# A kernel of two phases: centring products moved between the halves of a convolution, and a pair's ranks, numbers and weights moved ahead of the second normalisation of the step

## The chip, the cores and the metric

The kernel runs on one core of a Trainium2 chip. The metric is the device time of one execution in microseconds (us). Before the change it is 1603.58 us, the median of 3 runs (1603.55 to 1603.79).

## What is computed

The input is 32 images of 128 channels and 32x32 pixels. In the order of the reference:

```python
x = x + conv(ln_c(x))        # ln_c: normalise over the 128 channels of each pixel
# conv: 3x3 depthwise, its nine weights for each image and channel are a softmax of
#   (max(x) @ w2.T + b2) - (mean(x) @ w1.T + b1); plus bias, plus its own input
t = tokens(x)                # 32 * 1024 tokens of 128 numbers
t = t + experts(ln_t(t))     # top 2 of 8 experts, 128 -> 512 -> gelu -> 128, weighted by a softmax of the two gate logits
x = images(t)
```

The softmax of the nine weights runs over an axis of length 1, and the kernel carries it out like that. The convolution and the routing fill the first third of the time and the experts nearly all of the rest.

## The kernel before, in words

**First phase: 19 steps over 16 pairs of images.** A pair goes through four stages, one step apart, so that a step works on up to four pairs: stage n of step s handles pair s - n + 1. Steps 3 to 15 have all four stages. Every engine has its own `step` function, and the order of the calls in it is the order of its work; nothing else schedules it. Engines meet through semaphores only. In what follows image 0 and image 1 are the two of a pair, and an image's 1024 pixels are treated as two halves of 512.

- Stage 1, normalisation. (The **mark** of a step, below, is the variance product of the second half of its image 1: once per step.)
  PE (TensorE) subtracts the channel mean (`centre`, L745, into psA, one buffer of 1024 columns), ACT (ScalarE) squares (`square`, L540), PE averages (`variance`, L754, one half at a time into psVar, one buffer), ACT takes logarithm and exponential (`inv_std`, L547 and L551), DVE (VectorE) multiplies (`norm`, L1045), which also frees psA, and ACT sums the image up (`sum_up`, L556). DVE splits the pooled values in two (`split_pooled`, L1053 and L1054), PE multiplies them with the tap weights (`tap_logits`, 36 small products, L774 and L775), and DVE makes the taps (`tap_softmax`, L1064 to L1073, with an exponential on ACT at L652).
- Stage 2, convolution. ACT builds diagonal weights (`diagonals`, L564, five for image 0 and four for image 1). PE convolves with them (`conv`, L803, a half at a time into psConv, one buffer), ACT takes each half out (`take`, L572, tile cv). DVE adds the image (`add_image`, L1080) and the taps that PE doesn't do (`window`, L1090: four for image 0, five for image 1, the latter a stage later). `add_image` also frees the buffer xb, which SyncE then loads with the image four further on.
- Stage 3, tokens. PE transposes and multiplies with the gate (`turn`, L788 and L790, into psT, one buffer), ACT makes the token's standard deviation (`token_std`: L580, eight squares at L584, L588, L590) and stores the row (`keep`, L598 and L600), which frees psT. DVE scales the gate logits (`shifts`, L1104 and L1105).
- Stage 4, routing. DVE picks two experts (`first_choice`, `second_choice`, L1112 to L1144), PE counts ranks (`ranks`, L816 to L822), DVE makes row numbers (`place`, `number`, L1151 to L1163) and weights (`weigh`, L1170 to L1177). POOL (GpSimd) then scatters the 2048 rows of the pair to memory with 16 indirect DMAs (L464). Two tiles `rows` and two tiles `idx` alternate between pairs.

**Between the phases** DVE makes the table of tiles, SyncE and ACT write 29 blocks of padding rows (L330), PE and DVE shift the first weights (L884, L885, L1274, L1277), and SyncE loads the first sorted rows once all scatters and padding have landed.

**Second phase: 156 tiles of 256 rows.** PE does `up` (L920 to L922), `turn_rows` (L907) and `down` (L943, L944) for the two experts of a tile. `down` ends with the bias product for the two blocks of 128 rows (L947). A last phase turns the tokens back into images.

The function bodies that the steps below refer to follow.

## Time and profile before

| what | value |
|---|---|
| median of 3 runs | 1603.58 us |
| the profiled execution, its own time | 1603.79 us |
| its span in the profile | 1601.5 us |
| PE, DVE, ACT, POOL busy in the span | 92%, 85%, 67%, 60% |
| mean granted TensorE clock | 0.945 |
| first phase, to the last row number of pair 15 | 0 to 573 us |
| second phase, products of the experts | 617 to 1514 us |
| last phase | 1514 to 1601.5 us |

Time outside the span is 2.3 us. A busy share is an average over phases with different limits, so the page's first lines do not tell what sets the time of the first phase. For that the rows of single engines in order of time are needed: each gives start and duration in us, the engine, the line, the tiles, and in brackets how long the engine was idle before it and who ended that.

### The profile page before, as it was taken

How to read it: one execution, taken by the hardware profiler on the slowest of the kernel's cores; microseconds unless marked ns; L12 is line 12 of the kernel's file. 1: busy time of each engine (PE TensorE's matmuls, PEld its weight loads, DVE VectorE, ACT ScalarE, POOL GpSimd, SP SyncE). 2: the span in 40 equal slices, each digit the busy share in tenths (PEclk: the TensorE clock that was granted, in tenths of full speed). 3: DMA queues.
4: the chain of work that ended last, by engine and by line, in shares of the span. 5: the costliest groups of instructions: out<-in, count | busy, mean ns of one | idle time of the engine just before them, and what ended most of it. 6: DMA issues, size and time to landing. Idle time of an engine off the chain costs nothing.

```text
span 1601.5 us, 45597 instructions
## 1 busy us (share of the span) xinstructions
PE 1475.7 (92%) x12254; PEld 1135.7 (71%) x12255; DVE 1367.1 (85%) x2725; ACT 1070.1 (67%) x2410; POOL 966.4 (60%) x1061
## 2 busy tenths in 40 slices
PE   5899999999998677999999999999999999999766
PEld 2344545454545415999999999999999999999655
DVE  2568888888888856999999999999999999999654
ACT  4577777777776415777777777777777777777400
POOL 1004555456545674777777777777777777777500
PEclk7999999999999757999999999999999999999876
DMA  4201122222211173111111111111111111110199
GB/s 135 79 27 67 60 76 68 67 60 77 64 66 52 41 131 79 42 44 45 47 47 44 43 40 44 44 47 41 47 47 43 48 45 47 47 44 8 37 406 397
DMA packets 62200, 115.77 MB, mean 72 GB/s; under 512 B 15551, under 2 KB 39259, under 8 KB 62154
## 3 DMA queue, kind: packets, MB, share of 16 engines
q1 hardware_dynamic: 37354, 62.28, 13.1%
q0 software_dynamic: 18176, 34.27, 6.9%
q10 hardware_dynamic: 6624, 18.69, 3.3%
q8 instruction: 19, 0.31, 0.1%
q14 instruction: 27, 0.22, 0.1%
HBM read 60.22 MB, written 58.61 MB: 74 GB/s over the span
## 4 chain that ended last, share of the span: by engine, by line
POOL 34%; issue 23%; DMA 5%; POOLq 1%; PE 1%; DVE 1%; SPq 0%; ACT 0%
POOL token_out L488 16%; POOL xn L476 9%; POOL yt L483 8%; DMA ye<-token_out 4%; POOL rows_by_pair L464 1%; PE psV L982 1%; DMA rows_by_pair<-rows,idx 1%; POOLq L488 1%; POOLq L482 0%; POOLq L486 0%; PE psT L788 0%; POOLq L474 0%; POOLq L484 0%; DMA token_out<-yt,rt 0%; DMA rt<-rows_by_pair 0%
## 5 line engine op out<-in xcount | busy, mean ns | idle before, releaser
L1296 DVE TENSOR_TENSOR gl<-g,gh 128x512 f16<-128x512 f32 x624 | 515.1, 865 | 25.5 <-ACT gh L688 16.6
L488 POOL DMA_INDIRECT token_out<-yt,rt x312 | 377.8, 1211 | 186.5 <-POOL yt L483 132.7
L464 POOL DMA_INDIRECT rows_by_pair<-rows,idx x256 | 272.0, 1062 | 323.8 <-issue 200.1
L803 PE MATMUL psV<-lp,diag 128*128 128x512 f32 x576 | 275.1, 610 | 18.6 <-ACT cv L572 17.6
L688 ACT ACTIVATE gh<-g 128x512 f16<-128x512 f32 x468 | 276.2, 624 | 17.2
L681 ACT ACTIVATE g<-psT 128x512 f32<-128x512 f32 x312 | 183.1, 597 | 107.4 <-DVE gl L1296 67.1
L681 ACT ACTIVATE g<-psV 128x512 f32<-128x512 f32 x312 | 185.2, 597 | 91.7 <-PE psV L922 73.3
L943 PE MATMUL psR<-wall,gh 128*128 x1248 | 222.7, 273 | 0.6 <-DVE ya L1313 0.6
L943 PE MATMUL psG<-wall,gh 128*128 x1248 | 222.7, 273 | 0.0
L944 PE MATMUL psG<-wall,gl 128*128 x1248 | 214.3, 219 | 0.0
L944 PE MATMUL psR<-wall,gl 128*128 x1248 | 214.3, 219 | 0.0
L803 PEld LDWEIGHTS psV<-lp,diag 128*128 128x128 f32 x576 | 105.2, 192 | 147.5 <-issue 109.9
L476 POOL TENSOR_SCALAR xn<-rt 128x128 f32<-128x128 f32 x312 | 190.9, 625 | 14.1 <-DMA rt<-rows_by_pair 10.5
L1090 DVE SCALAR_TENSOR_TENSOR x<-lp,taps,x 128x1024 f32<-128x1024 f32 x144 | 184.7, 1283 | 3.5
L920 PE MATMUL psV<-xh,wall 128*128 128x256 f16 x624 | 170.7, 274 | 0.0
L921 PE MATMUL psV<-xl,wall 128*128 128x256 f16 x624 | 170.7, 274 | 0.0
L922 PE MATMUL psV<-xh,wall 128*128 128x256 f16 x624 | 170.7, 274 | 0.0
L921 PE MATMUL psT<-xl,wall 128*128 128x256 f16 x624 | 170.2, 273 | 0.0
L920 PE MATMUL psT<-xh,wall 128*128 128x256 f16 x624 | 170.2, 273 | 0.0
L922 PE MATMUL psT<-xh,wall 128*128 128x256 f16 x624 | 170.1, 273 | 0.0
L1313 DVE SCALAR_TENSOR_TENSOR ya<-psR,rt,ya 128x256 f32<-128x256 f32 x312 | 135.2, 474 | 1.0 <-PE psR L947 1.0
L483 POOL TENSOR_TENSOR yt<-ya 128x256 f32<-128x256 f32 x156 | 120.8, 774 | 23.1 <-DVE ya L1313 19.0
(210 smaller groups left out, 2969.9 us busy)
## 6 DMA issues: line engine op xcount, KB each, us to landing
rt<-rows_by_pair SPq DMA_DIRECT2D x156, 133.0 KB
xb<-in_x_dram SPq DMA_DIRECT2D x32, 512.0 KB, 3.5
ye<-token_out SPq DMA_DIRECT2D x32, 512.0 KB, 7.9
out_dram<-oe ACTq DMA_DIRECT2D x32, 512.0 KB, 8.5
token_out<-yt,rt POOLq DMA_INDIRECT x312
rows_by_pair<-rows,idx POOLq DMA_INDIRECT x256, 2.4
stage<-in_L_ffn_W_dram SPq DMA_DIRECT2D x1, 2048.0 KB, 8.5
rows_by_pair<-pad_rows SPq DMA_DIRECT2D x15, 133.0 KB, 9.7
```

The costliest lines, as they stand in the source:

```text
L464: gp.indirect_dma_start(rows_dram, bass.IndirectOffsetOnAxis(ap=idx[p][:, b:b + 1].bitcast(U32), axis=0), rows[p][:, b, :], None).then_inc ...
L476: last = gp.tensor_scalar(xn[q][:, b, :], rt[r % RING][:, b, 0:D], rt[r % RING][:, b, RSTD:RSTD + 1], rt[r % RING][:, b, NMR:NMR + 1], ALU ...
L488: gp.indirect_dma_start(y_dram, bass.IndirectOffsetOnAxis(ap=rt[r][:, b, ID:ID + 1].bitcast(U32), axis=0), yt[r][:, b, :], None, bounds_ch ...
L681: sc_.activation(g[side][:, cols], hbank[side][:, cols], ACT.Gelu, scale=1.0 / WSCALE).then_inc(g_done, 1)
L688: sc_.activation(gh[side][q][:, cols], g[side][:, cols], ACT.Copy).then_inc(hi_act, 1)
L803: ins = te.matmul(psConv.rearrange("p (h w) -> p h w", w=WW), diag[k][:, m, :], lp[j][:, y:y + HH // 2, dx:dx + WW], start=(m == 0), stop= ...
L920: te.matmul(out_, high, xh[r % 4][:, :], start=True, stop=False)
L921: te.matmul(out_, high, xl[r % 4][:, :], start=False, stop=False)
L922: last = te.matmul(out_, wall[:, bass.ds(w + (O_1L + s * P), P)], xh[r % 4][:, :], start=False, stop=True)
L943: te.matmul(bank[:, 2 * b * D:2 * (b + 1) * D], gh[side][q][:, lhs], both, start=(s == 0 and b == 0), stop=False, skip_group_check=True)
L944: te.matmul(bank[:, 2 * b * D:(2 * b + 1) * D], gl[side][q][:, lhs], high, start=False, stop=False, skip_group_check=True)
L1296: v.tensor_tensor(gl[side][q][:, cols], g[side][:, cols], gh[side][q][:, cols], ALU.subtract).then_inc(lo_done, 1)
```

## The change

Everything but the last two points concerns the first phase.

- PE: the second `centre` of a step (image 1) moves from behind both convolution halves of image 0 to between them. `centre` of the next pair's image 0 moves from among the tap products to between the convolution halves of image 1. The first variance product of the next step moves to this step's end. `ranks` moves from behind the first half of image 1's convolution to ahead of it. The tap products are no longer interleaved with other products.
- ACT: `square` of image 1, `inv_std`, `sum_up` and `take` change places; the eight squares of image 1's tokens are split in four and four, around `inv_std` and `take`; `inv_std` of the first half now comes ahead of the diagonals; `keep` of image 1 comes behind `sum_up`.
- DVE: `place`, `number` and `weigh` go together ahead of the second `norm`, and `split_pooled` right behind it. All four taps of image 0 follow. In steps 17 and 18, which have no convolution, the choice of experts comes first (`early`).
- The last pair has a third `rows` tile, a third `idx` tile and two semaphores of its own, so that it doesn't wait for the scatter of pair 13.
- Second phase: the two bias products of `down` become one of 256 columns with a broadcast operand.

The core of the diff (the class Step, POOL, the steps of ACT and of PE in their new order, `down`, and the step of DVE; the old order of ACT and PE stands in the functions above):

```diff
+            def last(self, stage):
+                return self.fixed and 2 * self.t + self.r - (stage - 1) == NU - 1
+            def row_slot(self, stage):
+                return 2 if self.last(stage) else self.slot(stage)
...
+            def scatter(p):
+                pool.reg_alu(routed, routed, 1, ALU.add)
+                pool.reg_alu(images, images, 2, ALU.add)
+                pool.wait_ge(s_const, 3)
+                pool.wait_ge(routed_ready, routed)
+                pool.wait_ge(kept, images)
+                for b in range(NB2):
+                    gp.indirect_dma_start(rows_dram, bass.IndirectOffsetOnAxis(ap=idx[p][:, b:b + 1].bitcast(U32), axis=0),
+                                          rows[p][:, b, :], None).then_inc(rows_out[2 * p + b // NBLK], 16)
+            with pool.Fori(0, NU // 2 - 1, 1) as t:
                 for p in range(2):
-                    pool.reg_alu(routed, routed, 1, ALU.add)
-                    pool.reg_alu(images, images, 2, ALU.add)
-                    pool.wait_ge(s_const, 3)
-                    pool.wait_ge(routed_ready, routed)
-                    pool.wait_ge(kept, images)
-                    for b in range(NB2):
-                        gp.indirect_dma_start(rows_dram, bass.IndirectOffsetOnAxis(ap=idx[p][:, b:b + 1].bitcast(U32), axis=0),
-                                              rows[p][:, b, :], None).then_inc(rows_out[2 * p + b // NBLK], 16)
+                    scatter(p)
+            scatter(0)
+            scatter(2)
...
+                if st_.on(1):
+                    inv_std(st_, 0, 0)
                 if st_.on(2):
                     diagonals(st_, 0)
-                for k in range(2):
...
+                if st_.first:
+                    for n in range(2, 4):
+                        high_taps(n)
+                if st_.on(1):
+                    inv_std(st_, 0, 1)
+                if st_.on(2):
+                    diagonals(st_, 1)
+                if st_.first:
+                    for n in range(4, 6):
+                        high_taps(n)
+                    gate_bias()
+                if st_.on(1):
+                    sum_up(st_, 0)
+                if st_.on(2):
+                    take(st_, 0, 0)
+                if st_.first:
+                    high_w2(0, E // 2)
+                if st_.on(3):
+                    token_squares(st_, 0, 0, NBLK)
+                    token_std(st_, 0)
+                    keep(st_, 0)
+                if st_.on(1):
+                    square(st_, 1)
+                if st_.first:
+                    high_w2(E // 2, E - 2)
+                if st_.on(2):
+                    take(st_, 0, 1)
+                if st_.on(1):
+                    inv_std(st_, 1, 0)
+                if st_.first:
+                    high_w2(E - 2, E)
+                if st_.on(4):
+                    expose(st_)
+                if st_.on(3):
+                    token_squares(st_, 1, 0, NBLK // 2)
+                if st_.on(1):
+                    inv_std(st_, 1, 1)
+                if st_.on(2):
+                    take(st_, 1, 0)
+                if st_.on(3):
+                    token_squares(st_, 1, NBLK // 2, NBLK)
+                    token_std(st_, 1)
+                if st_.first:
+                    high_b2()
+                if st_.on(1):
+                    sum_up(st_, 1)
+                if st_.on(3):
+                    keep(st_, 1)
                 if st_.next().on(1):
                     square(st_.next(), 0)
-                if st_.on(1):
+                if st_.on(2):
+                    take(st_, 1, 1)
+                if st_.on(1):
...
-                    for h in range(2):
-                        centre(st_, 0, h)
+                    centre_both(st_, 0)
...
+                    variance(st_, 0, 0)
+                    for n in range(2, 4):
+                        turn_weights(n)
+                if st_.on(3):
+                    turn(st_, 0)
+                if st_.on(1):
+                    variance(st_, 0, 1)
+                if st_.first:
+                    for n in range(4, 6):
+                        turn_weights(n)
+                    gate_products()
+                if st_.on(2):
+                    conv(st_, 0, 0, 0, len(taps_pe[0]))
+                if st_.on(1):
+                    centre_both(st_, 1)
+                if st_.on(2):
+                    conv(st_, 0, 1, 0, len(taps_pe[0]))
+                elif st_.on(4):
+                    ranks(st_)
+                if st_.on(3):
+                    turn(st_, 1)
+                if st_.on(1):
+                    variance(st_, 1, 0)
+                if st_.on(2) and st_.on(4):
+                    ranks(st_)
+                if st_.on(2):
+                    conv(st_, 1, 0, 0, 2)
+                if st_.on(1):
+                    variance(st_, 1, 1)
+                if st_.on(2):
+                    conv(st_, 1, 0, 2, N_PE)
+                if st_.next().on(1):
+                    centre_both(st_.next(), 0)
+                if st_.on(2):
+                    conv(st_, 1, 1, 0, N_PE)
...
+                if st_.on(1):
+                    tap_logits(st_)
+                if st_.next().on(1):
+                    variance(st_.next(), 0, 0)
...
                 bias = wall[:, bass.ds(w + O_B2, D)]
-                for b in range(TB):
-                    last = te.matmul(bank[:, 2 * b * D:(2 * b + 1) * D], bias_sel[:, :], bias, start=False, stop=(b == TB - 1), skip_group_check=True)
-                last.then_inc(y_ready, 1)
+                te.matmul(bank.rearrange("p (b n d) -> p b n d", n=2, d=D)[:, :, 0, :], bias_sel[:, :], bias.unsqueeze(1).broadcast_to([P, TB, D]),
+                          start=False, stop=True, skip_group_check=True).then_inc(y_ready, 1)
...
             def step(st_):
+                early = st_.on(4) and not st_.on(2)
+                if early:
+                    first_choice(st_)
+                    second_choice(st_)
                 if st_.on(3):
-                    window(st_, 3, 1, 0, 3)
...
-                    window(st_, 3, 1, 3, N_DVE)
-                if st_.on(4):
+                    window(st_, 3, 1, 2, N_DVE)
+                if st_.on(4) and not early:
                     first_choice(st_)
                     second_choice(st_)
                 if st_.on(2):
                     add_image(st_, 0)
-                    window(st_, 2, 0, 0, 2)
-                if st_.on(1):
-                    norm(st_, 1)
                 if st_.on(4):
                     place(st_)
-                if st_.on(1):
+                    number(st_)
+                    weigh(st_)
+                if st_.on(1):
+                    norm(st_, 1)
                     split_pooled(st_)
-                if st_.on(4):
-                    number(st_)
-                if st_.on(4):
-                    weigh(st_)
                 if st_.on(2):
-                    window(st_, 2, 0, 2, 3)
+                    window(st_, 2, 0, 0, N_DVE - 1)
                 if st_.on(3):
                     shifts(st_)
-                if st_.on(2):
-                    window(st_, 2, 0, 3, N_DVE - 1)
                 if st_.on(1):
                     tap_softmax(st_)
                 if st_.on(2):
```

Where the order moves, on the engines that wait for each other there. On ACT, in the loop's second step, image 1 of each stage, the order before (psV is the bank of both psVar and psConv, pooled the sums, spent the discarded squares):

```order
L547 ACTIVATE lnv<-psV,eps_c 128x512
L551 ACTIVATE sd<-lnv 128x512
L572 ACTIVATE cv<-psV,conv_b 128x512
L556 ACTIVATE sq,pooled<-lp 128x1024
L580 ACTIVATE negm<-psG 128x8
L584 ACTIVATE spent,ssq<-psT,negm 128x128 x8
L588 ACTIVATE tln<-ssq,eps_t 128x8
L590 ACTIVATE rstd<-tln 128x8
L598 ACTIVATE rows<-psT 128x8x128
L600 ACTIVATE rows<-rstd 128x8
L572 ACTIVATE cv<-psV,conv_b 128x512
```

And now, the same stretch:

```order
L560 ACTIVATE lnv<-psV,eps_c 128x512
L564 ACTIVATE sd<-lnv 128x512
L585 ACTIVATE cv<-psV,conv_b 128x512
L598 ACTIVATE spent,ssq<-psT,negm 128x128 x4
L607 ACTIVATE tln<-ssq,eps_t 128x8
L609 ACTIVATE rstd<-tln 128x8
L569 ACTIVATE sq,pooled<-lp 128x1024
L617 ACTIVATE rows<-psT 128x8x128
L619 ACTIVATE rows<-rstd 128x8
```

The sum of image 1 (L556, now L569) stood right behind the `take` of the first half; now half of the token squares and the deviation stand between them.

On DVE, around the second `norm` of a step in the loop, before:

```order
L1045 ISA lp,pooled<-psA,sd 128x32x32
L1045 ISA pooled 128x1
L1151 TENSOR_TENSOR pos<-psR,base 128x448
L45 REGISTER_ALU
L1152 TENSOR_TENSOR base<-base,psR 128x28
L1050 REGISTER_ALU
L1053 CAST pool<-pooled 128x2x2
L45 ISA
L1054 TENSOR_TENSOR pool<-pooled,pool 128x2x2
```

And now:

```order
L1215 TENSOR_SCALAR rows<-rows 128x16
L1080 ISA
L1083 ISA lp,pooled<-psA,sd 128x32x32
L1083 ISA pooled 128x1
L1088 REGISTER_ALU
L1091 CAST pool<-pooled 128x2x2
```

`place` stood between the norm and the split of the pooled values (L1053, now L1091); nothing stands there any more.

On PE, step 1, which has no routing and no tokens and so shows the plain order, before:

```order
L754 MATMUL psV<-sq,mean_w 128x512
L803 MATMUL psV<-lp,diag 128x512 x2
L754 MATMUL psV<-sq,mean_w 128x512
L803 MATMUL psV<-lp,diag 128x512 x8
L745 MATMUL psA<-xb,centre_w 128x512 x2
L754 MATMUL psV<-sq,mean_w 128x512
L803 MATMUL psV<-lp,diag 128x512 x2
L754 MATMUL psV<-sq,mean_w 128x512
L803 MATMUL psV<-lp,diag 128x512 x5
```

And now:

```order
L791 MATMUL psV<-sq,mean_w 128x512 x2
L838 MATMUL psV<-lp,diag 128x512 x5
L782 MATMUL psA<-xb,centre_w 128x512 x2
L838 MATMUL psV<-lp,diag 128x512 x5
L791 MATMUL psV<-sq,mean_w 128x512
L838 MATMUL psV<-lp,diag 128x512 x2
L791 MATMUL psV<-sq,mean_w 128x512
L838 MATMUL psV<-lp,diag 128x512 x2
L782 MATMUL psA<-xb,centre_w 128x512 x2
L838 MATMUL psV<-lp,diag 128x512 x4
```

Both variance products of image 0 now come ahead of its convolution, its two halves are parted by `centre` of image 1, and those of image 1 by `centre` of the next pair.

## Rows read from the trace of the kernel before

**Rows 1.** Stretch, length, busy PE, PEld, DVE, ACT, POOL, PEclk, DMA share, GB/s

```profile
123.35:502.75 379.40, 354.39 (x1705) 189.48 (x1704) 324.64 (x781) 287.52 (x852) 207.10 (x192) 1.00 0.21 68
```

**Rows 2.** PE in order of time, from the mark of one step to the next

```profile
313.04 1.02 PE L754 MATMUL psV<-sq,mean_w 128*128 128x512 f32 x2
...
315.62 0.35 PE L816 MATMUL psR<-pairs,tri_b 128*128 128x448 bf16 x1
...
316.56 2.84 PE L803 MATMUL psV<-lp,diag 128*128 128x512 f32 x6 [0.19 <-ACT cv L572]
...
324.20 1.12 PE L754 MATMUL psV<-sq,mean_w 128*128 128x512 f32 x2 [1.09 <-ACT sq L540]
...
333.70 4.56 PE L803 MATMUL psV<-lp,diag 128*128 128x512 f32 x10 [0.85 <-ACT cv L572]
...
343.01 1.88 PE L803 MATMUL psV<-lp,diag 128*128 128x512 f32 x4
344.73 1.02 PE L754 MATMUL psV<-sq,mean_w 128*128 128x512 f32 x2
```

**Rows 3.** ACT in order of time, the same step

```profile
315.81 0.69 ACT L572 ACTIVATE cv<-psV,conv_b 128x512 f32<-128x512 f32 x1 [0.37 <-PE psV L803]
316.86 1.06 ACT L556 ACTIVATE sq<-lp 128x1024 f32<-128x1024 f32 x1 [0.35 <-DVE pooled L1045]
...
318.10 0.37 ACT L584 ACTIVATE spent<-psT,negm 128x128 f32<-128x128 f32 x1
...
320.51 0.40 ACT L584 ACTIVATE spent<-psT,negm 128x128 f32<-128x128 f32 x1
...
321.48 1.01 ACT L598 ACTIVATE rows<-psT 128x1024 f32<-128x1024 f32 x1
...
324.28 0.22 ACT L652 ACTIVATE ez<-zd 128x18 f32<-128x18 f32 x1 [0.21 <-DVE zd L1067]
325.73 1.57 ACT L564 ACTIVATE diag<-ident,taps 128x128 f32<-128x128 f32 x5 [1.23 <-DVE taps L1073]
...
328.52 1.26 ACT L564 ACTIVATE diag<-ident,taps 128x128 f32<-128x128 f32 x4
```

**Rows 4.** DVE in order of time, the same step

```profile
315.59 1.23 DVE L1045 CUSTOM_DVE_ANT_0 lp<-psA,sd 128x1024 f32<-128x1024 f32 x1 [1.14 <-ACT sd L551]
...
318.04 0.17 DVE L1053 CAST pool<-pooled 128x4 f16<-128x4 f32 x1 [0.46 <-ACT sq L556]
...
320.66 1.27 DVE L1090 SCALAR_TENSOR_TENSOR x<-lp,taps,x 128x1024 f32<-128x1024 f32 x1
...
323.45 0.17 DVE L1064 SCALAR_TENSOR_TENSOR zt<-psR,cbd 128x18 f32<-128x18 f32 x1
```

**Rows 5.** PE in order of time: the mark of step 1

```profile
60.51 1.02 PE L754 MATMUL psV<-sq,mean_w 128*128 128x512 f32 x2
```

**Rows 6.** PE in order of time: start of step 16, after its wait

```profile
513.20 0.33 PE L788 MATMUL psT<-ident,x 128*128 128x128 f32 x1 [2.27 <-DVE x L1090]
...
514.41 0.46 PE L788 MATMUL psT<-ident,x 128*128 128x128 f32 x1
```

**Rows 7.** DVE and PE in order of time: steps 17 and 18, last image

```profile
542.63 6.57 DVE L1090 SCALAR_TENSOR_TENSOR x<-lp,taps,x 128x1024 f32<-128x1024 f32 x5
...
555.82 0.17 DVE L1144 TENSOR_TENSOR gaps<-gap,gaps 128x16 f32<-128x16 f32 x1
...
553.96 0.45 PE L788 MATMUL psT<-ident,x 128*128 128x128 f32 x1 [8.08 <-ACT rows L600]
...
573.02 2.05 PE L884 MATMUL psA<-stage,ones 128*128 128x512 f32 x2 [2.43 <-DVE idx L1163]
```

**Rows 8.** The chain that ended last, between the phases: start us, us, what

```profile
602.86 7.16 DMA rows_by_pair<-rows,idx
```

**Rows 9.** PE in order of time, second phase: bias products and what follows

```profile
700.91 0.28 PE L947 MATMUL psR<-wall,bias_sel 128*128 x2
701.02 0.27 PE L920 MATMUL psV<-xh,wall 128*128 128x256 f16 x1
```

More of the change, by code:

```diff
@@ L250, in conv_moe_block @@
         cv = [sb(f"cv{k}", [P, PIX], held=phase_a) for k in range(2)]
-        rows = [sb(f"rows{p}", [P, NB2, RW], held=phase_a) for p in range(2)]
+        rows = [sb(f"rows{p}", [P, NB2, RW], held=phase_a) for p in range(3)]
         phase_a.close()
@@ L433, in _ @@
             gp.memset(zero28[:, :], 0.0)
-            for p in range(2):
-                gp.iota(rows[p][:, :, ID].rearrange("p (k b) -> p k b", k=2).bitcast(I32), [[PIX, 2], [1, NBLK]], base=(2 * p - 4) * PIX,
+            for p, pair in enumerate((0, 1, NU - 1)):
+                gp.iota(rows[p][:, :, ID].rearrange("p (k b) -> p k b", k=2).bitcast(I32), [[PIX, 2], [1, NBLK]], base=(2 * pair - 4) * PIX,
                         channel_multiplier=NBLK)
@@ L592, in keep @@
             def keep(st_, k):
-                p = st_.slot(3)
-                if not st_.fixed or st_.turns(3) > 0:
+                p = st_.row_slot(3)
+                if not st_.fixed or (st_.turns(3) > 0 and not st_.last(3)):
                     act.wait_ge(rows_out[2 * p + k], 16 * NBLK * st_.turns(3))
@@ L791, in turn, with conv @@
                 last.then_inc(tok_ready, 1)
-            def conv(st_, k, h, m):
+            def conv(st_, k, h, first, end):
                 j = 2 * st_.slot(2) + k
-                if m == 0:
+                if first == 0:
                     if h == 0:
```

149 lines of the change are left out of this document (43 added, 106 removed).

## The prediction

> **What bounds the kernel now.** I read the busy time by stretch first, then single engines in order of time, then the chain that ended last. The twelve full steps from the mark of step 3, at 123.35, to that of step 15, at 502.75, take 379.40 us, 31.62 each, at full clock [rows 1]. PE is busy 354.39 of it and DVE 324.64, so none of the engines is full: a loop through several of them sets the step. In one step [rows 2 to 4] the loop is this. The mark at 313.04 leads to `norm` of image 1 at 315.59, that to `sum_up` on ACT at 316.86, then eight token squares, the deviation, `keep`, `take` and `square`, until the first variance product of the next step at 324.20, before which PE stood 1.09 us; from there PE runs to the first half of the next convolution, waits 0.85 us for `take` [rows 2], and reaches the next mark at 344.73, 31.69 later. DVE waits 1.14 us before this `norm` and 0.46 us before the split [rows 4].
>
> Behind the first phase DVE, PE, ACT's padding and POOL's scatters meet: the last scatter is issued at 602.86 and lands 7.16 us later [rows 8]. The second phase is full on PE, as the bias rows show, where each product starts when the last one's columns are through [rows 9].
>
> **The step, part by part.** Removed: the wait of 1.09 us, since `square` of the next image no longer stands behind `take`, and PE now has its own work between the two `take`s of image 0, which removes the 0.85 us. Nothing of the arithmetic goes; the split squares cost no extra instruction. So I ask which loop closes next. In the new order `sum_up` of image 1 stands on ACT behind `take`, four squares and the deviation, and on DVE the split has nothing ahead of it to cover its wait. From the mark:
> - `take` starts 2.77 later (313.04 to 315.81) and holds ACT 0.6 of its 0.69. Eight squares start 0.344 apart ((320.51 - 318.10)/7) and, with the deviation, take 3.38 to `keep` at 321.48; with four fewer 2.00. `sum_up` starts at 5.37 [rows 2, 3].
> - `sum_up` to split takes 1.18 (316.86 to 318.04). The split is two small instructions, 0.28: DVE starts the taps at 6.83. `norm` ended at 2.55 + 1.23 = 3.78, so DVE stands about 2.8 us where it stood 0.46 [rows 3, 4].
> - Two taps and `shifts` took 2.79 (320.66 to 323.45); two more at 1.31 (6.57/5 [rows 7]) make 5.41: `tap_softmax` starts at 12.24 [rows 4].
> - The exponential follows 0.83 later (323.45 to 324.28) and takes 0.13 of ACT; `inv_std` of the first half and five diagonals took 2.79 together in the other order (325.73 to 328.52); with their tail and the wake-up of PE 0.15. The convolution starts at 16.14 [rows 3, 4].
> - A half, `centre`, `turn` and the first variance product of image 1 took 9.31 (333.70 to 343.01). The second half is ten pieces at 0.43 (1.72/4, 343.01 to 344.73), 4.3; `ranks` at most 0.75 (315.62 to 316.56 less the wait of 0.19); two taps 1.72. The next mark is at 16.14 + 16.08 = 32.2 [rows 2].
>
> So the new loop is 32.2 us, **0.6 longer** than now, although two waits went. The other loops are shorter: DVE's own, 31.62 less both norms' waits (about 1.2 each) and the 0.46, is about 28.8 of work, plus the 2.8 of standing: 31.6. ACT's `keep` of image 0 and `turn` of image 1 have about 0.6 to spare, `ranks` 0.4. Twelve steps: +7.0.
>
> **The start.** In step 0 `centre` of the next pair no longer stands behind tap products, and in step 1 the second variance product of image 0 comes directly behind the first instead of behind two convolution taps; the mark of step 1 at 60.51 should come at about 56.6 [rows 5]. Steps 1 and 2 lack the routing, step 1 also the squares that delay the split. Carried through with the durations above, the mark of step 3 is about 118.4 instead of 123.35 [rows 1], **-5**. I bound it by 0 (the cold clock takes it back) and -7.
>
> **The end.** From the mark of step 15 to `tap_softmax` and all that follows it was 10.41 (313.04 to 323.45) and is now 12.24: +1.83 [rows 2, 4]. In step 17 the choice (6.8, from the taps' end at 549.20 to 555.99) now stands ahead of the five taps of the last image (6.57), and `turn` waits for these; before, it stood 8.08 and started at 553.96, 4.8 after the taps' end, for the row tile that the third one now replaces [rows 7]. So 4.8 of the 6.8 are covered and 2.0 are not, and `add_image` before it comes 0.6 earlier: +1.3 (bounds 0 and 2). The last row number, now 572.9 (PE follows at 573.02 [rows 7]), comes 7.0 - 5 + 1.8 + 1.3 = 5.1 later. The padding starts with it and keeps the DMA engines full until the last scatter lands [rows 8]; POOL's scatters of pairs 14 and 15 run back to back and are some 0.9 us earlier to their places, which leaves about 0.7 us less to move. The second phase starts about 4.4 later.
>
> **The second phase.** The bias pair and its successor start 0.11 apart [rows 9]; that is 256 columns, 0.107 us at 2.4 GHz, so one product of 256 columns costs the same but for a few ns. With 0.01 of rounding each of the 312 merges gives back 0 to 6 ns: 0 to 2 us, and I take -0.5. Bounds: 0, and -17 if the one product cost what one of the two does (0.055 x 312). A broadcast operand is nothing new: four of the six products of `ranks` have one, and 1,372 columns go through in 0.75 at most [rows 2].
> The Trainium skill, "TensorE: Matmul & The Clock Gate", section "Back-to-back issue gap", gives about 81 ns as the sustained spacing at 128 columns in a real stream of weight loads and products; by that the pair costs 162 ns and the merge could give back 53 ns each, -16.5 in all. Rows 9 speak against it: 110 ns for both.
>
> **Sum.** +7.0 - 5 + 1.8 + 1.3 - 0.7 - 0.5 = +3.9, against the profiled execution's 1603.79: 1607.7; the median of the runs is 0.2 lower: **1607.5 us**. That is 0.2% slower, and about 0.2% (3.2 us) is what a measurement of this kernel can tell from no change. An error of 0.1 us in the loop is 1.2 us of the time; this case alone spans 1602 to 1613.
>
> **Rivals.**
> - *Faster: the split hardly waits.* If PE reaches the mark 1.5 us sooner than DVE reaches `norm`, ACT has the squares behind it and `sum_up` follows `norm` at once; the split then waits 1.2 instead of 2.8, and the step is about 28.8 + 1.2 + 0.5 = 30.5. Then 13 steps give back 1.7 each: 1607.5 - 22 = 1585. For it: both waits of PE [rows 2] go. Against it: the PE part of the loop, 16.08 us, has no wait left to give. 12%.
> - *Faster or the same: the loop is 31.6.* If my terms are 0.6 too long, only start and end count: 1600. 10%.
> - *Slower: the clock.* PE will stand 1.1 us for `norm` and 1.2 us for `shifts`, with only small products between. After standing 2.27 us PE's transposes went from full speed to 1.2 GHz at 514.41 [rows 6]. If that came in each step, `turn` and a half would take 2.5 to 3.4 us more, over twelve steps 30 to 40: about 1640. Against it: now PE stands 1.09 and 0.85 and the granted clock is 1.00 [rows 1]. 5%.
> - *Slower: images late.* `add_image` comes closer to the `centre` that needs the buffer, about 4.9 us. If that became a wait of 1 us, the step grows as much: 1619. The load has some 1 us to spare. 3%.
> - *Faster: one narrow product's price for the merged bias,* by rows 9 at most -17: 1590. The page cited above points that way. 3%.
>
> **The numbers.** My case has 62%, the rivals 33%, and 5% is for what I don't see. Of my case's 62, 42 lie above 1606.8, 19 within 3.2 us of before, 1 below. With the rivals (slower 8; faster 12 + 3 + 5, the same 5) and the rest spread: slower 0.46, within 0.2% 0.30, faster 0.24. The range 1590 to 1614 leaves out 1585, 1619 and 1640, 20% together.
>
> **What would show it.** Marks 32.2 apart in steps 3 to 15; DVE standing about 2.8 us before the split, released by ACT's sum; no wait of PE for `square` or for `take` of image 0, but one of 1.1 us before `centre` of the next pair; the mark of step 3 near 118; the padding about 5 us later; the second phase as long as before. The steps are wrong if the marks are 31 us or less apart, or the granted clock falls below 1 in steps 3 to 15.

## The result, and the profile after

The changed kernel takes **1629.6 us** (median of 4 runs, 1624.6 to 1632.9), against 1603.57 for the kernel before (4 runs, 1602.25 to 1603.79): ratio 1.0165, 95% interval 1.0146 to 1.0183. It is 1.65% slower, where 0.2% slower was forecast, and it lies outside the range of 1590 to 1614.

The page of the profiled execution (1630.09 us, span 1628.3) gives a first hint of the place. Each digit of PEclk is the mean granted TensorE clock of one fortieth of the span, in tenths, and a 9 stands for 90% or more. The row of the kernel before, and then the page after:

```profile
PEclk7999999999999757999999999999999999999876
```

```profile
PE 1499.2 (92%) x11942; PEld 1148.0 (71%) x11943; DVE 1367.6 (84%) x2725; ACT 1069.5 (66%) x2410; POOL 970.2 (60%) x1062
...
PEclk7999989999899955999999999999999999999976
```

Slices 4 to 13 are the steps of the first phase. All of them stand at 9 before; after, two stand at 8. The stretches tell it plainly: the twelve steps from the mark of step 3 (120.91) to that of step 15 (530.39), and two single steps (columns as in [rows 1]):

```profile
120.91:530.39 409.48, 379.21 (x1705) 205.75 (x1704) 325.86 (x781) 285.48 (x854) 210.31 (x192) 0.92 0.19 63
292.12:324.19 32.07, 29.40 (x144) 15.52 (x142) 26.35 (x65) 23.64 (x73) 17.21 (x16) 1.00 0.20 65
324.19:359.19 35.00, 32.48 (x144) 17.43 (x142) 27.95 (x67) 23.88 (x73) 16.33 (x16) 0.90 0.23 74
```

They take 409.48 us instead of 379.40 [rows 1], 34.12 each, at a mean clock of 0.92 instead of 1.00. One step of the twelve, 292.12 to 324.19, kept the full clock: it took **32.07**. The next one fell to 0.90 and took 35.00. That step on PE in order of time, answering to [rows 2]:

```profile
324.19 1.02 PE L791 MATMUL psV<-sq,mean_w 128*128 128x512 f32 x2
...
328.02 1.98 PE L782 MATMUL psA<-xb,centre_w 128*128 128x512 f32 x4 [1.10 <-DVE pooled L1083]
329.85 3.60 PE L838 MATMUL psV<-lp,diag 128*128 128x512 f32 x8
333.28 0.17 PE L809 MATMUL psR<-pool,cwT 128*128 128x4 f16 x1
...
334.18 1.10 PE L791 MATMUL psV<-sq,mean_w 128*128 128x512 f32 x2
336.71 0.33 PE L822 MATMUL psT<-ident,x 128*128 128x128 f32 x1 [1.42 <-DVE lg L1143]
336.87 0.29 PE L824 MATMUL psG<-wgc,x 128*128 128x9 f32 x2
...
338.79 0.45 PE L822 MATMUL psT<-ident,x 128*128 128x128 f32 x1
339.04 0.44 PE L824 MATMUL psG<-wgc,x 128*128 128x9 f32 x2
...
339.86 2.06 PE L791 MATMUL psV<-sq,mean_w 128*128 128x512 f32 x2
341.70 6.04 PE L838 MATMUL psV<-lp,diag 128*128 128x512 f32 x10
...
359.19 1.02 PE L791 MATMUL psV<-sq,mean_w 128*128 128x512 f32 x2
```

The waits before the variance product and before the second half's convolution are gone. Instead PE works through 36 tap products in one piece from 333.28, does one variance product, and stands 1.42 us. `turn` starts at full speed (0.33 and 0.29), and by 338.79 the same products take 0.45 and 0.44; the variance product takes 2.06 instead of the 1.10 before the wait, and the ten products of the convolution's first half take 6.04, where ten such products took 4.56 [rows 2]. ACT and DVE in the same step, answering to [rows 3, 4]:

```profile
326.96 0.69 ACT L585 ACTIVATE cv<-psV,conv_b 128x512 f32<-128x512 f32 x1 [0.37 <-PE psV L838]
...
329.53 1.04 ACT L569 ACTIVATE sq<-lp 128x1024 f32<-128x1024 f32 x1
...
337.33 0.22 ACT L689 ACTIVATE ez<-zd 128x18 f32<-128x18 f32 x1 [3.16 <-DVE zd L1105]
```

```profile
326.74 1.23 DVE L1083 CUSTOM_DVE_ANT_0 lp<-psA,sd 128x1024 f32<-128x1024 f32 x1 [0.24 <-ACT sd L564]
...
330.69 0.17 DVE L1091 CAST pool<-pooled 128x4 f16<-128x4 f32 x1 [2.72 <-ACT sq L569]
...
331.01 1.33 DVE L1128 SCALAR_TENSOR_TENSOR x<-lp,taps,x 128x1024 f32<-128x1024 f32 x1
...
336.50 0.16 DVE L1102 SCALAR_TENSOR_TENSOR zt<-psR,cbd 128x18 f32<-128x18 f32 x1
```

The split waits 2.72 us for the sum of image 1, taps begin at 331.01, 6.82 behind the mark, and `tap_softmax` at 336.50, 12.31 behind it.

Where the 26.8 us of span went, profile against profile: the mark of step 3 comes 2.4 earlier (120.91 against 123.35), the twelve steps take 30.1 longer, from the mark of step 15 to the last row number it is 2.8 more (72.8 against 69.95), from there to the first product of the second phase 3.0 less (41.4 against 44.4), and the second phase with the last one 0.6 less.

### The profile page after: what moved, and what is told of

Its sections match the earlier page's. It is cut to its first block, busy times and chain, and to the rows that moved or that the text cites. A ratio compares the mean times of both kernels' runs of the same rounds, so it can differ in the third digit from the quotient of the medians.

```text
span 1628.3 us, 44961 instructions
## 1 busy us (share of the span) xinstructions
PE 1499.2 (92%) x11942; PEld 1148.0 (71%) x11943; DVE 1367.6 (84%) x2725; ACT 1069.5 (66%) x2410; POOL 970.2 (60%) x1062
## 4 chain that ended last, share of the span: by engine, by line
POOL 32%; PE 25%; issue 24%; DVE 7%; DMA 6%; ACT 4%; POOLq 1%; SPq 1%; ACTq 0%; DVEq 0%
POOL token_out L501 16%; PE psV L838 13%; POOL xn L489 9%; POOL yt L496 8%; DVE x L1128 4%; DMA out_dram<-oe 4%; PE psV L791 3%; PE psT L822 3%; PE psG L824 2%; PE psA L782 2%; ACT spent L598 1%; DMA stage<-in_L_ffn_W_dram 1%; DMA rows_by_pair<-pad_rows 1%; ACT cv L585 1%; DVE oe L1382 1%
## 5 line engine op out<-in xcount | busy, mean ns | idle before, releaser
L471 POOL DMA_INDIRECT rows_by_pair<-rows,idx x256 | 275.7, 1077 | 345.1 <-issue 230.0
L838 PEld LDWEIGHTS psV<-lp,diag 128*128 128x128 f32 x576 | 113.2, 200 | 150.8 <-issue 138.3
```

What stands on the lines that cost most here:

```text
L471: gp.indirect_dma_start(rows_dram, bass.IndirectOffsetOnAxis(ap=idx[p][:, b:b + 1].bitcast(U32), axis=0), rows[p][:, b, :], None).then_inc ...
L838: ins = te.matmul(psConv.rearrange("p (h w) -> p h w", w=WW), diag[k][:, m, :], lp[j][:, y:y + HH // 2, dx:dx + WW], start=(m == 0), stop= ...
```

## The experiments

Two theories stood behind the first of them. **A: the clock falls because TensorE stands still ahead of `turn`.** **B: it falls because the 36 narrow tap products now stand in one piece beside that wait.** A third question was whether the loop that I had worked out (sum, split, taps, softmax, diagonals, convolution) really sets the step. A fourth group takes single parts of the change.

### Tap products apart again

```diff
                 if st_.on(2):
-                    conv(st_, 1, 1, 0, N_PE)
+                    conv(st_, 1, 1, 0, 2)
...
-                if st_.on(1):
-                    tap_logits(st_)
-                if st_.next().on(1):
-                    variance(st_.next(), 0, 0)
+                for quarter in range(4):
+                    if st_.on(1):
+                        tap_logits(st_, quarter)
+                    if st_.on(2) and quarter < 2:
+                        conv(st_, 1, 1, 2 + quarter, 3 + quarter)
+                    if quarter == 2 and st_.next().on(1):
+                        variance(st_.next(), 0, 0)
```

> The changed kernel, with the 36 tap products of a step in four groups again, between the last two products of each convolution and ahead of the next variance product, one group behind it. Theory A (the clock falls because TensorE stands some 1.25 us for DVE ahead of turn): nothing changes, marks about 34.1 apart, 1628 to 1631. Rival B (it falls because 36 narrow products stand in one piece right ahead of that wait): the granted clock stays at 1.00 in most steps, marks 32.1 apart, 12 x 2 us less: about 1605.

Measured: 1622.4 us, ratio 1.0128 (1.0111 to 1.0145). The twelve steps:

```profile
119.62:521.73 402.11, 372.41 (x1705) 199.43 (x1704) 326.58 (x782) 285.08 (x854) 208.64 (x192) 0.95 0.20 64
```

33.5 each, between the two forecasts: the clock still falls, in fewer steps (eight of the twelve took 33.3 us or more, instead of eleven; mean 0.95 instead of 0.92). Parting the piece gives back 0.6 of the 1.9 us that a step had lost (the full loss follows from the next run). The last group of twelve tap products still stands directly ahead of the wait, as in the kernel before, and PE stands there 1.1 to 1.3 us, little more than the 1.0 to 1.1 us of the kernel before, whose clock stays at 1.00. So the piece matters, but it is not the whole.

### A wide product in the wait

```diff
+                if k == 0:
+                    if not st_.fixed or st_.count(3, 2, 0) > 0:
+                        pe.wait_ge(kept, st_.count(3, 2, 0))
+                    te.matmul(psT[:, 0:512].rearrange("p (b d) -> p b d", d=P), ident[:, :],
+                              ident[:, :].unsqueeze(1).broadcast_to([P, 4, P]), start=True, stop=True)
                 pe.wait_ge(x1_ready, st_.count(3, 2, k + 1))
```

> The changed kernel plus one product of 512 columns, whose result is written over, ahead of turn of image 0: it lies in the wait of 1.25 us and delays nothing as long as it takes some 0.9 us. Theory A (the fall comes from the wait): clock 1.00 through steps 3 to 15, marks 32.1 to 32.2 apart instead of 34.1, and 12 x 2 + 2.7 us less: about 1603. Rival B (narrow products, which stay): mostly as the changed kernel, 1620 or more. Rival C (the fall comes with the wait of 1.2 us before centre): as the changed kernel, 1629.

Measured: 1603.9 us, ratio 1.0012 (1.0002 to 1.0022). The wait in one step (first row: the added product), and then the twelve steps:

```profile
352.60 1.02 PE L819 MATMUL psT<-ident 128*128 128x512 f32 x2
354.00 0.33 PE L826 MATMUL psT<-ident,x 128*128 128x128 f32 x1 [0.38 <-DVE lg L1147]
```

```profile
115.87:502.51 386.64, 363.04 (x1730) 191.22 (x1728) 324.87 (x781) 283.94 (x854) 201.52 (x192) 1.00 0.20 67
```

One product per step that nobody reads gives back 1.5% of the kernel's time. The steps take 32.22 each at a clock of 1.00: the 32.2 of the prediction. The fall is the whole of what the prediction missed. The wait of 1.1 to 1.2 us before `centre`, which is rival C above, is still in every step here, so it does not bring the clock down by itself.

### Narrow products in the wait

The same place, with 30 products of 4 columns in place of the wide one:

```diff
-                    te.matmul(psT[:, 0:512].rearrange("p (b d) -> p b d", d=P), ident[:, :],
-                              ident[:, :].unsqueeze(1).broadcast_to([P, 4, P]), start=True, stop=True)
+                    for n in range(30):
+                        te.matmul(psT[:, 4 * n:4 * n + 4], cwT[:, 0, 0, 0, :], ident[:, 0:4].bitcast(F16)[:, 0:4], start=True, stop=True)
```

> The changed kernel, with the wait before turn of image 0 filled by 30 products of 4 columns each (about 0.8 us, results written over) instead of one of 512 columns. Theory A (the fall comes from TensorE standing still): it no longer stands, clock 1.00, marks 32.2 apart, 1604 as with the wide product. Theory B (the fall comes from a stretch in which few columns go through, standing or narrow alike): nothing helps, it falls as in the changed kernel, marks 34 to 35 apart, 1626 to 1640.

Measured: 1626.4 us, ratio 1.0133 (1.0109 to 1.0156).

```profile
368.25 0.89 PE L820 MATMUL psT<-ident,cwT 128*128 128x4 f16 x30
369.72 0.33 PE L827 MATMUL psT<-ident,x 128*128 128x128 f32 x1 [0.57 <-DVE lg L1148]
```

```profile
119.11:528.52 409.41, 388.16 (x2065) 216.24 (x2064) 326.04 (x781) 285.45 (x854) 211.05 (x192) 0.92 0.20 63
```

PE now stands 0.57 instead of 1.42 us and is busy for 388.16 us of the twelve steps, more than with the wide product (363.04), and the clock falls as before: 34.12 a step. Theory A in its plain form is out: it is not the standing alone. Time filled with narrow products did not help, about the same time filled with a wide one did.

### Half a product in the wait

The wide product cut to 256 columns.

```diff
-                    te.matmul(psT[:, 0:512].rearrange("p (b d) -> p b d", d=P), ident[:, :],
-                              ident[:, :].unsqueeze(1).broadcast_to([P, 4, P]), start=True, stop=True)
+                    te.matmul(psT[:, 0:256].rearrange("p (b d) -> p b d", d=P), ident[:, :],
+                              ident[:, :].unsqueeze(1).broadcast_to([P, 2, P]), start=True, stop=True)
```

> The changed kernel with a product of 256 columns (0.43 us) in the wait ahead of turn, half of the one that kept the clock up. If what counts is how many columns go through around the wait: between the two, falls in some steps, marks 32.3 to 33.3 apart, 1605 to 1617. If any real work in the wait is enough: 1604. If it must be filled: 1625 and more.

Measured: 1606.9 us, ratio 1.0045 (1.003 to 1.006).

```profile
117.33:506.17 388.84, 360.76 (x1730) 192.93 (x1729) 325.29 (x781) 284.42 (x854) 203.44 (x192) 0.99 0.21 67
```

The steps take 32.4 each, near the lower forecast: the first and the fifth of the twelve took 33.3, the others 32.0 to 32.6. PE stands 0.8 to 1.1 us before `turn` here, longer than the 0.5 to 0.8 us beside the 30 narrow products, and yet it keeps its clock in most steps. That leaves little of the rival that the narrow products failed only because some wait was left.

### The kernel before, with its tap products in one piece

If B is right, the kernel before can be broken in the same way without adding a wait. Only the loop over quarters changes: the four pieces of convolution and `centre` first, then all tap products.

```diff
                         centre(st_.next(), 0, quarter - 2)
-                    if st_.on(1):
-                        tap_logits(st_, quarter)
+                if st_.on(1):
+                    for quarter in range(4):
+                        tap_logits(st_, quarter)
```

> The kernel before, with its 36 tap products in one piece behind both centre products, ahead of the variance product that waits 1.09 us. Theory A: a wait of 1.1 us behind narrow products differs little from before, the clock stays, 1603 to 1606. Rival B (narrow products in one piece next to a wait bring the clock down): it falls in most steps, about 2 us each, 1625.

Measured: 1645.8 us, ratio 1.0275 (1.0257 to 1.0292), the slowest of all.

```profile
344.23 2.07 PE L754 MATMUL psV<-sq,mean_w 128*128 128x512 f32 x2 [1.36 <-ACT sq L540]
346.09 0.42 PE L788 MATMUL psT<-ident,x 128*128 128x128 f32 x1
```

```profile
120.35:544.08 423.73, 395.45 (x1705) 219.15 (x1704) 324.28 (x781) 287.79 (x852) 207.56 (x192) 0.89 0.19 61
```

The wait before the variance product is 1.36 where it was 1.09 [rows 2], and behind it the products run at about half speed (2.07 instead of 1.12, 0.42 instead of 0.27). The steps take 35.3, so each lost 3.7 us, nearly twice what B had forecast. The edit changed two things at this place: all 36 tap products now stand right ahead of the wait instead of twelve, and the wait itself is 0.27 us longer. No run tells the two apart.

The same with a product of 512 columns put ahead of that variance product:

```diff
                 for k in range(2):
+                    if k == 0 and st_.on(1) and st_.on(3):
+                        if not st_.fixed or st_.count(3, 2, 0) > 0:
+                            pe.wait_ge(kept, st_.count(3, 2, 0))
+                        te.matmul(psT[:, 0:512].rearrange("p (b d) -> p b d", d=P), ident[:, :],
+                                  ident[:, :].unsqueeze(1).broadcast_to([P, 4, P]), start=True, stop=True)
                     if k == 0 and st_.on(1):
                         variance(st_, k, 0)
```

> The kernel before with its tap products in one piece (1645.8 us), and a product of 512 columns in the wait of 1.28 us behind them. If the clock fell there too because little goes through the array around that wait: clock 1.00, marks 31.6 to 31.9 apart, 1603 to 1607. If narrow products in one piece are costly in another way (marks 3.7 further apart for some other reason): it stays above 1630.

```profile
120.19:499.59 379.40, 363.11 (x1730) 192.61 (x1728) 324.63 (x781) 287.49 (x852) 207.13 (x192) 1.00 0.21 68
```

Measured: 1597.3 us, ratio 0.9987 (0.9978 to 0.9996), and the twelve steps take 379.40, to the hundredth what they took before. So the fall is all that the piece of narrow products had cost in these steps; they come 3.2 us earlier, because the mark of step 3 is at 120.19 instead of 123.35, as it is in the run without the wide product (120.35). The wait that is left behind the wide product is 0.3 us.

### The sum of image 1 first

```diff
                 if st_.on(2):
                     take(st_, 1, 0)
+                if st_.on(1):
+                    sum_up(st_, 1)
                 if st_.on(3):
                     token_squares(st_, 1, NBLK // 2, NBLK)
                     token_std(st_, 1)
...
-                if st_.on(1):
-                    sum_up(st_, 1)
```

> The changed kernel with the sum of image 1 on ACT directly behind take, ahead of the second four token squares. If my loop is right (sum, split, taps, tap_softmax, diagonals, convolution) the sum comes 1.5 us earlier, DVE stands 1.2 instead of 2.7 us before the split, the wait of TensorE before turn nearly goes, the clock stays at 1.00 and the marks are 30.6 to 31.0 apart: 12 x 3.3 us less, about 1588 to 1592. If another loop closes at once (DVE's own, or ACT's), marks at 31.6 and more: 1600. If the fall of the clock has nothing to do with the wait: 1610.

Measured: **1581.6 us, ratio 0.9875** (0.9858 to 0.9891): faster than both kernels.

```profile
332.27 1.23 DVE L1083 CUSTOM_DVE_ANT_0 lp<-psA,sd 128x1024 f32<-128x1024 f32 x1 [0.58 <-ACT sd L564]
...
334.72 0.17 DVE L1091 CAST pool<-pooled 128x4 f16<-128x4 f32 x1 [1.22 <-ACT sq L569]
...
335.04 5.25 DVE L1128 SCALAR_TENSOR_TENSOR x<-lp,taps,x 128x1024 f32<-128x1024 f32 x4
...
340.49 0.17 DVE L1102 SCALAR_TENSOR_TENSOR zt<-psR,cbd 128x18 f32<-128x18 f32 x1
```

```profile
114.43:483.35 368.92, 351.02 (x1706) 186.96 (x1705) 325.18 (x781) 285.60 (x854) 209.18 (x192) 1.00 0.22 70
```

The split waits 1.22 instead of 2.72, all that follows on DVE is 1.5 us earlier against `norm`, `turn` hardly waits, the clock stays at 1.00, and the steps take 30.7. The 36 tap products still stand in one piece here: without the wait ahead of `turn`, the piece does no harm. The time is 6 us below the forecast of 1588 to 1592, most of it because the start gained too (mark of step 3 at 114.43 instead of 120.91), which the forecast had left out. The loop of the prediction is the one that sets the step: a change at one point of it moved the step by what it had been said to (32.2 less 1.5).

### Numbers and weights behind the split again

On top of the last kernel, with the order that DVE had before the change:

```diff
                 if st_.on(4):
-                    place(st_)
-                    number(st_)
-                    weigh(st_)
+                    if not st_.on(1):
+                        place(st_)
                 if st_.on(1):
                     norm(st_, 1)
+                if st_.on(4):
+                    if st_.on(1):
+                        place(st_)
+                if st_.on(1):
                     split_pooled(st_)
+                if st_.on(4):
+                    number(st_)
+                    weigh(st_)
```

> The kernel with the sum of image 1 first (1581.6 us), with the row numbers and weights on DVE behind split_pooled again, place between norm and split as before the change. By my loop norm stays where ACT lets it start, place (0.8 us) is hidden in the wait of 1.2 us for the sum, and numbers and weights (2.4 us) push taps, tap_softmax and the next convolution back: marks 2.3 further apart, 33.0, and 1581.6 + 12 x 2.3 = 1609 at full clock, up to 1635 if TensorE's longer wait before turn brings the clock down. Rival: what is gone ahead of norm lets it start earlier by as much: 1582 to 1586.

```profile
325.24 1.23 DVE L1083 CUSTOM_DVE_ANT_0 lp<-psA,sd 128x1024 f32<-128x1024 f32 x1 [4.33 <-ACT sd L564]
...
327.69 0.17 DVE L1091 CAST pool<-pooled 128x4 f16<-128x4 f32 x1 [0.46 <-ACT sq L569]
...
330.30 5.24 DVE L1128 SCALAR_TENSOR_TENSOR x<-lp,taps,x 128x1024 f32<-128x1024 f32 x4
...
335.75 0.17 DVE L1102 SCALAR_TENSOR_TENSOR zt<-psR,cbd 128x18 f32<-128x18 f32 x1
```

```profile
114.14:527.10 412.96, 374.22 (x1705) 200.02 (x1704) 324.43 (x780) 286.64 (x854) 208.03 (x192) 0.94 0.19 63
```

Measured: 1628.9 us, ratio 1.0174 (1.0154 to 1.0194), 47 us more than with the numbers ahead of `norm`, inside the forecast of 1609 to 1635. `norm` does not start earlier for it: DVE stood 4.33 us for ACT's deviation at 325.24. From the split at 327.69 to the taps it is now 2.61 instead of 0.32 (334.72 to 335.04 in the kernel above), as forecast; PE then stands 2.1 us before `turn` and the clock is 0.94. The forecast for full clock was 33.0 a step, and 34.4 were measured. So moving the numbers and weights ahead of `norm` is worth much in this order, because it fills a time in which DVE would stand. By this forecast 2.3 of the 3.7 us that a step lost are the loop and 1.4 the clock; that split is an estimate, since no run has this order at full clock.

### Parts of the change alone, on the kernel before

The last pair's own tiles (on POOL, ACT, SyncE and DVE as in the change) and the early choice of experts:

```diff
+                early = st_.on(4) and not st_.on(2)
+                if early:
+                    first_choice(st_)
+                    second_choice(st_)
                 if st_.on(3):
                     window(st_, 3, 1, 0, 3)
...
-                if st_.on(4):
+                if st_.on(4) and not early:
                     first_choice(st_)
                     second_choice(st_)
...
-                    if k == 1 and st_.on(4):
+                    if st_.on(4) and k == (1 if st_.on(2) else 0):
                         ranks(st_)
```

> The kernel before, with only the last pair's own row and index tiles and the early choice of experts in steps 17 and 18. By the terms of my prediction: last row number 2.0 us later than 572.9 (choice of 6.8 us ahead of the taps, 4.8 gained at turn), 0.7 less of scatters behind it: 1.3 us slower at most, 1603 to 1605. By the trace of the changed kernel, where the start of the second phase moved 3.1 us less than the last row number did: 1 to 2 us faster.

The tiles without the lines above:

> The kernel before, with only the last pair's own row and index tiles, the choice of experts in its old place. turn of the last image then starts when its taps are done, 4.8 us earlier than 553.96, but DVE's choices follow each other as before: the last row number comes 2 to 4.8 us earlier, and the whole is 2 to 6 us faster than before: 1597 to 1601. If what follows is set by the padding and the scatters alone: within 1 us of before.

The rows of the row numbers (sixteen, first and last start in us), first of the kernel before, then with both, then with the tiles alone:

```profile
L1163 DVE SCALAR_TENSOR_TENSOR idx<-idf x16: 174/176/177, 129.9 to 572.7; 128x16 int32<-128x16 f32 x16
```

```profile
L1176 DVE SCALAR_TENSOR_TENSOR idx<-idf x16: 174/176/177, 130.2 to 574.8; 128x16 int32<-128x16 f32 x16
```

```profile
L1176 DVE SCALAR_TENSOR_TENSOR idx<-idf x16: 174/176/178, 129.2 to 569.3; 128x16 int32<-128x16 f32 x16
```

Both: 1602.9 us, ratio 0.9999 (0.999 to 1.0009). Tiles alone: 1599.7, ratio 0.9978 (0.9969 to 0.9988). With both, the last row number comes at 574.8, 2.1 later than before (2.0 counted from the mark of step 15), where the prediction had 2.0; with the tiles alone it comes at 569.3, 3.4 earlier (2.7 counted from that mark). The early choice takes back what the third tile gives.

The merged bias product alone:

```diff
-                for b in range(TB):
-                    last = te.matmul(bank[:, 2 * b * D:(2 * b + 1) * D], bias_sel[:, :], bias, start=False, stop=(b == TB - 1), skip_group_check=True)
-                last.then_inc(y_ready, 1)
+                te.matmul(bank.rearrange("p (b n d) -> p b n d", n=2, d=D)[:, :, 0, :], bias_sel[:, :], bias.unsqueeze(1).broadcast_to([P, TB, D]),
+                          start=False, stop=True, skip_group_check=True).then_inc(y_ready, 1)
```

> The kernel before, with only the two bias products of down merged into one of 256 columns. By the trace of the changed kernel (first to last bias row 881.0 instead of 881.9 us): 0.9 us faster, ratio 0.9994, which is inside of what can be told. By one narrow product's duration (0.055 us for each of 312): 17 us faster, 1586.

```profile
L946 PE MATMUL psG<-wall,bias_sel x156: 272/273/273, 621.1 to 1502.1; 128*128 x156
```

Measured: 1598.4 us, ratio 0.9989 (0.998 to 0.9998). From the first of these rows to the last it is 881.0 us; in the kernel before, 881.9 (624.0 to 1505.9). 0.9 us, as the changed kernel has it:

```profile
L985 PE MATMUL psG<-wall,bias_sel x156: 272/273/273, 652.0 to 1533.0; 128*128 x156
```

The profile with the merged bias product also shows how far the stretch between the phases moves by itself: its first phase is that of the kernel before (mark of step 15 at 502.83), and from its last row number (573.0) to the second phase it is 41.0 us, not the 44.4 of the profile before. In the other profiled runs it is 40.8 to 44.1. The 3.0 us that seemed won there are therefore not shown to be an effect of the change.

### The best of both

The sum of image 1 first, as above, and no early choice:

```diff
-                early = st_.on(4) and not st_.on(2)
+                early = False
...
-                elif st_.on(4):
-                    ranks(st_)
                 if st_.on(3):
                     turn(st_, 1)
                 if st_.on(1):
                     variance(st_, 1, 0)
-                if st_.on(2) and st_.on(4):
+                if st_.on(4):
                     ranks(st_)
```

> The kernel with the sum of image 1 first (1581.6 us), without the early choice of experts in steps 17 and 18. If the early choice costs what it did alone (1602.9 against 1599.7): the last row number 5 us earlier, 3 us less in all, 1578 to 1579. Rival: with POOL's scatters now closer behind, the choice of pair 14 is late for POOL and the scatters end as before: 1581 to 1582.

Measured: **1577.9 us, ratio 0.9862** (0.9847 to 0.9877), against 0.9875 with the early choice. The kernel before was measured again beside each group of experiments, with medians of 1602.4, 1603.15 and 1599.7, so the ratios are what compares: 1.4% faster than before. The intervals of the two ratios overlap, so the gain over the early choice is seen only in the profiles: from the mark of step 15 to the last row number it is 68.0 us instead of 71.5.

## Why the prediction was wrong

**The loop: right.** 32.2 was forecast for a step, 32.07 was measured in the one step at full clock and 32.22 as the mean with the wide product. The terms hold singly: taps 6.82 behind the mark (6.83), `tap_softmax` 12.31 (12.24), the start of the convolution 16.06 in the step at full clock (16.14), the wait of the split 2.72 (2.8), PE's wait for `norm` 1.10 (1.1) and for DVE ahead of `turn` 1.24 in the step at full clock (1.2), up to 1.53 in the others.

**The clock: the step that failed.** The prediction's loop took TensorE to keep its full clock in the new waits. It did not: in eleven of the twelve steps the granted clock was 0.90 or 0.95, and that added 1.9 us a step, 22.8 us in all. The fall stood among the rivals, with its place and its cause, at 5%. The argument against it, "now PE stands 1.09 and 0.85 and the granted clock is 1.00", compared only the length of the waits, and the new ones are longer (up to 1.53). What lay beside them was left out: before, the tap products stood in groups of 8 to 12 with 1.1 us of wide ones between them; after, all 36 stand together, one variance product follows, then the wait. Putting the narrow products together brought the clock down in the kernel before as well, at a wait of 1.3 us. In the changed kernel parting them gave back a third of the loss; filling the wait with a wide product, or taking the wait away, gave back all of it. The prediction listed this move ("with only small products between") and gave it no chance of its own. Its price was put too high: 2.5 to 3.4 us in each of twelve steps, against 1.90 on average (34.12 - 32.22): one step was spared, four took 33.3 to 33.5, and the other seven 34.7 to 35.0, 2.5 to 2.8 more than 32.22.

**The start: right in kind, the exact hit luck.** The mark of step 1 came at 56.52 (56.6 forecast). But the runs with another product ahead of `turn`, which change nothing before step 2, have it at 53.56 to 55.45, so this mark moves by some 3 us of itself, and the start's term can't be checked more closely than that. The step that ends at the mark of step 3 was the first to lose its clock and took 34.8 instead of 32.0 with the wide product, so that only 2.4 of the 5 arrived; with the wide product the mark of step 3 was at 115.87, which is 7.5 earlier, beyond the bound of 7.

**The end.** +1.8 and +1.3 were forecast from the mark of step 15 to the last row number, +2.8 was measured; the part of 2.0 for the early choice was 2.0 by itself, counted from the mark. The 0.7 us of backlog can't be told from what that stretch varies by. [rows 8] do not show that the padding keeps the DMA engines full, on which that term rests; by the trace their busy share is 1.01 from 573 to 602.86, so it does up to the last scatter, and 0.57 while that lands.

**The second phase.** -0.5 forecast, -0.9 measured, of 312 merges. The section of the Trainium skill that spoke for -16.5 ("TensorE: Matmul & The Clock Gate", "Back-to-back issue gap") is answered by the trace: two products of 128 columns, each with its weight load, took 110 ns together [rows 9], where the figure of that section makes an estimated 162, and merging gave back 3 ns a pair.

**The sum without the clock.** 1607.5, range of that case 1602 to 1613. The changed kernel with the wide product measured 1.0012 of the kernel before, 1605.5: that case was sized rightly, and the clock added the 1.5% between 1.0012 and 1.0165.

**The chances** do not add up: by the prediction's own list 42 and 8 make 50% for slower by more than 0.2%, before anything is spread, where it says 46%.

## What to carry to other kernels

When an edit regroups TensorE's work, list for each wait what stands next to it, not only how long it is: 36 narrow products in one piece beside a wait of 1.3 us cost this kernel 2.75%, where the same products in four groups, with wide ones between them, and a wait of 1.1 us did no harm. Where the order can't be changed, a wide product that nobody reads, put into a wait that exists anyway, is a cheap test for such a loss, and here it gave back all that the clock had cost. And a move that leaves a new wait on an engine should be read to its end: one call moved on ACT, the sum ahead of four squares, turned 1.65% slower into 1.25% faster.

## What the runs showed of the hardware

- TensorE's granted clock fell to its lower level (1.2 GHz) for part of a step and came back by itself within the step. A mean of 0.90 means a fifth of the step at half speed, and 0.95 a tenth, so seven steps of 34.9 us at 0.90 and four of 33.3 us at 0.95 make an estimated 0.2 x 7 x 34.9 + 0.1 x 4 x 33.3 = 62 us at half speed. The twelve steps became 23 us longer by it.
- Being busy by the profile doesn't protect. With narrow products in the wait PE was busy 388 of 409 us (95%) and fell; with the wide one 363 of 387 (94%) and did not fall. The same holds close to the fall: in one step of the run with narrow products PE was busy 5.73 of the last 6.30 us before the clock fell (91%, 364.00 to 370.30), while in the kernel before it was busy 4.87 of the 5.96 us that end 1 us behind the wait of 1.09 us (82%, 319.20 to 325.16), and the clock did not fall. The Trainium skill, "TensorE: Matmul & The Clock Gate", section "Part 1: The HAM clock gate (the "warmup" mystery)", says that the clock follows how busy the engine has been of late; if busy is read as the profile's busy row, this trace disagrees.
- The same program loses a different amount from step to step (32.07 to 35.02 us, clock 0.90, 0.95 or 1.00), though its instructions are the same in each. From run to run it took 1624.6 to 1632.9, a spread of 0.5% over four runs; that this spread comes from the clock is not shown, since the kernel before with its tap products in one piece, which loses more, has 0.2% over four.
- What exactly makes the clock fall is not settled. The runs vary what lies in the wait and beside it (nothing, 30 products of 4 columns, 256 and 512 columns), and in the changed kernel neither the piece of narrow products without the wait nor the wait filled with a wide product brings the clock down. No run varies the length of the wait alone.
